# Latents' attention: the scaled copies of the keys made by ScalarE instead of VectorE

## What is computed

```python
x = x + xattn(ctx_1024, layernorm(x))   # 64 latents look at 1601 tokens and themselves, 16 heads of 64
x = x + attn(layernorm(x))              # differential attention of the latents
x = x + ffn(layernorm(x))               # 8 experts, top 2, softmax gates
```

```python
Q, K, V = (X @ W.T).reshape(b, n, 16, 16) ...   # each split in two halves of 8: Q1, Q2, K1, K2
attn = softmax(causal(Q1 K1' / sqrt(8))) - lam * softmax(causal(Q2 K2' / sqrt(8)))
O = rms_norm(attn @ V) * rms_scale * 0.2
out = O @ Wo.T
```

## Time and profile before

| | |
|---|---|
| median of three runs | 954.18 us (952.11 to 957.75) |
| the profiled execution | 957.0 us, of it a span of 955.3 us |
| TensorE busy | 914.2 us (96%) |
| VectorE busy | 800.5 us (84%) |
| ScalarE busy | 701.9 us (73%) |
| GpSimd busy | 378.7 us (40%) |
| mean granted clock of TensorE | 0.983 of full |

### The profile page before, as it was taken

The page is one execution under the profiler, slowest core; times in us unless marked ns, Lnnn a source line. Parts: engine busy times, 40 slices in busy tenths (PEclk is TensorE's granted clock), DMA queues, the critical chain, the costliest instruction groups (busy, mean ns, idle before and its releaser), DMA issues.

```text
span 955.3 us, 20495 instructions
## 1 busy us (share of the span) xinstructions
PE 914.2 (96%) x8246; PEld 491.1 (51%) x8246; DVE 800.5 (84%) x1591; ACT 701.9 (73%) x1003; POOL 378.7 (40%) x378
## 2 busy tenths in 40 slices
PE   8679999999999999999999999999999999999977
PEld 5444444545454545454545454545454545567653
DVE  5979797979798989898989898989897876498986
ACT  4756878787878787878787878787878677664633
POOL 6472034343434343434343434343434231354443
PEclk9889999999999999999999999999999999999987
DMA  6403030303030303030303030303020200000000
GB/s 213 83 1 71 1 93 2 93 2 75 22 74 21 74 22 73 22 73 22 73 23 72 23 72 24 73 23 72 23 60 23 38 23 24 1 24 24 2 2 22
DMA packets 74565, 41.95 MB, mean 44 GB/s; under 512 B 62276, under 2 KB 69864, under 8 KB 74472
## 3 DMA queue, kind: packets, MB, share of 16 engines
q1 hardware_dynamic: 74184, 39.60, 16.9%
q10 hardware_dynamic: 288, 1.05, 0.3%
HBM read 25.98 MB, written 0.59 MB: 28 GB/s over the span
## 4 chain that ended last, share of the span: by engine, by line
PE 81%; DVE 13%; ACT 3%; issue 2%; DMA 1%; POOL 0%; DVEq 0%; ACTq 0%
PE S L2141 10%; PE S L2132 9%; PE OA L2165 9%; PE OA L2168 9%; PE OA L2171 9%; PE S L2135 9%; PE WW L2075 8%; PE S L1217 2%; PE WW L2102 1%; PE WW L2103 1%; PE WW L2104 1%; DVE amx L802 1%; PE WW L2062 1%; PE WW L2063 1%; PE WW L2064 1%
## 5 line engine op out<-in xcount | busy, mean ns | idle before, releaser
L1849 ACT ACTIVATE region<-S,sigma 128x1024 f16<-128x1024 f32 x208 | 231.8, 1114 | 137.7 <-PE S L2141 137.7
L1530 DVE TENSOR_TENSOR region<-S,region 128x1024 f16<-128x1024 f32 x208 | 252.3, 1213 | 44.2 <-ACT S L1853 44.1
L1518 DVE TENSOR_REDUCE mx<-WW 128x1 f32<-128x512 f32 (+1 forms) x480 | 262.4, 583 | 29.7 <-PE WW L2075 22.4
L1853 ACT ACTIVATE S<-S,sigma 128x1024 f32<-128x1024 f32 x208 | 224.5, 1079 | 0.0
L1662 POOL TENSOR_TENSOR xk<-raw,xk 128x508 f16<-128x508 f32 x64 | 63.3, 999 | 168.1 <-DVE xk L1397 168.1
L2075 PE MATMUL WW<-xT,region 128*128 128x512 f16 x360 | 124.8, 381 | 4.4 <-DVE region L1509 2.1
L2132 PE MATMUL S<-region,xT 128*128 128x512 f16 (+1 forms) x416 | 124.5, 380 | 2.4 <-DVE region L1530 1.7
L2165 PE MATMUL OA<-region,xk 128*128 128x512 f16 (+1 forms) x416 | 123.8, 379 | 0.0
L2135 PE MATMUL S<-region,xT 128*128 128x512 f16 (+1 forms) x416 | 123.7, 379 | 0.0
L2141 PE MATMUL S<-region,xT 128*128 128x512 f16 (+1 forms) x416 | 123.7, 379 | 0.0
L2168 PE MATMUL OA<-region,xk 128*128 128x512 f16 (+1 forms) x416 | 123.7, 379 | 0.0
(11 more groups left out here) (314 smaller groups left out, 1836.6 us busy)
## 6 DMA issues: line engine op xcount, KB each, us to landing
raw<-ctx SPq DMA_DIRECT2D x16, 768.0 KB
rb<-inv_dram SPq DMA_DIRECT2D x16, 512.0 KB, 3.7
xT<-xk SPq DMA_TRANSPOSE x48, 3.1
left_row<-left_pT SPq DMA_DIRECT2D x48, 2.0 KB
raw<-ctx SPq DMA_DIRECT2D x16, 32.5 KB
WO_lo<-L_xattn_Wq ACTq DMA_DIRECT2D x1, 512.0 KB, 3.8
WO_hi<-L_xattn_Wkv ACTq DMA_DIRECT2D x1, 512.0 KB, 4.7
lx<-x SPq DMA_DIRECT2D x1, 512.0 KB, 7.1
```

Source lines behind the costliest of these rows:

```text
L1518: nc.vector.tensor_reduce(mx[:, r, c:c + 1], W[BANK[("m", n)]][:, 0:width], AX.X, ALU.max)\
L1530: nc.vector.tensor_tensor(p_lo[k], src, p_hi[k], ALU.subtract).then_inc(lo_done.sem, 1)
L1849: nc.scalar.activation(p_hi[k], src, ACT.Exp, scale=sigma[:, 0:1])
L1853: nc.scalar.activation(src, src, ACT.Exp, scale=sigma[:, 0:1]).then_inc(e_done.sem, 1)
```

## The change

In the six turns m = 0 to 5, VectorE no longer makes `Kx` of tile m+2. ScalarE does, right behind its copy of the queries, in four activations: each reads the 256 columns of keys from PSUM and multiplies them by one column of `pick` as a scale of one value per row. They wait for the projection and, from tile 2 on, for the scores of the tile whose buffer they overwrite. The keys of tiles 0 and 1 stay on VectorE. Nothing else moves.

```diff
+        def spread_keys(act, t):
+            wait(act, "projqk", t)
+            if t.off >= 2:
+                act.wait_ge(ta["scores"].sem, ta["scores"].upto(t.plus(-2), 1))
+            for k in range(4):
+                ins = nc.scalar.activation(Kx[t.off % 2][:, :, k, :],
+                                           W[0][:, 256:512].rearrange("p (c n) -> p c n", c=2), ACT.Copy,
+                                           scale=pick[:, k:k + 1])
+            ins.then_inc(ta["kx"].sem, 1)
+
@@ tail_vector
                 if m + 1 < TB:
                     maxima(t.plus(1), 0)
-                if m + 2 < TB:
-                    keys(dve, t.plus(2), W[0][:, 256:512])
                 if m == TB - 1:
@@ tail_scalar
                 if m + 2 < TB:
                     queries(act, t.plus(2), W[0][:, 0:256])
+                    spread_keys(act, t.plus(2))
                 if 0 < m < TB - 1:
                     values(act, t.plus(1), W[1])
```

## The result

| | before | changed kernel |
|---|---|---|
| median | 956.96 us (951.53 to 959.46, 22 runs) | 953.34 us (950.68 to 958.37, 22 runs) |
| the profiled execution | 957.0 us, span 955.3 | 951.6 us, span 949.9 |
| runs above 955.5 us | 13 of 22 | 2 of 22 |

The ratio is 0.9969 (95%: 0.9955 to 0.9982): 0.31% or 3.0 us faster, inside the forecast range and short of the 0.5% that counts as faster. But the two profiled spans differ by 5.4 us, the medians by 3.6 and the forecast was 1.5, so the number alone says little about the mechanism. The 22 times of before lie in two groups, 951.5 to 954.2 and 956.1 to 959.5, none between; 955.5 us is a line that I drew in the gap.

What follows compares the result with a forecast made beforehand. In the attention, TensorE and VectorE were taken as both full, with gains only where VectorE made TensorE idle. Gains of 1.16 + 0.21 + 0.61 = 1.98 less 0.5 gave 1.5 us off 954.18: 952.7 us, range 949.5 to 956.5.

Steps and rivals of the forecast that it cites:

- the clock's case: Rival, chance 0.14: TensorE's clock fall in the experts moves or vanishes; 5.4 us less (947), or 955 to 956.
- Turn 1 is worth 0.4: Attention turn 1: VectorE's L840 can begin 0.4 us earlier, then waits for GpSimd; turn 2 keeps the 0.4.
- turn 2's term of 1.16: Attention turn 2: with the keys early, TensorE's weigh_values is no longer held and L1179 begins 1.16 us earlier.
- the new bound: Attention turn 2: TensorE's next bound is ScalarE's copies 2 and 3, at 864.23 before and 0.4 us earlier now.
- Turns 4 and 5, 0.21 + 0.61: TensorE's wait of 0.21 us for Kx in turn 4 and of 0.61 for ScalarE's xk in turn 5 go away.
- Turn 3 gives nothing, VectorE waits 0.5 and 0.8: Attention turn 3: TensorE has no idle time, so no gain; VectorE waits 0.5 us for scores, 0.8 for weigh_values.
- The price of the spread, 0.364 each: ScalarE's new activations in the attention: 0.364 us each, 1.46 for four, each 0.47 to 0.50 long.
- The cost, 3 x 0.16 = 0.5: Attention turns 3, 4 and 5: ScalarE's late copy 0 holds TensorE 0.16 us a turn, 0.5 us in all.
- in turns 0 to 2 it falls into waits: Attention turns 0 to 2: the 0.16 us from ScalarE's lateness falls into TensorE's or VectorE's waits.
- ScalarE as the bound: Rival, chance 0.15: activations cost 0.575 us, TensorE is held 1.0 in turns 3 to 5; 956.4 us.
- VectorE as the bound all through: Rival, chance 0.06: every spread from turn 1 to 5 comes off, 5.65 us in all; 948.5 us.

Runs made afterwards that it cites:

- turn 1 alone: Kernel before, with ScalarE spreading the keys in turn 1 only and VectorE in the others: one run, 959.2 us.
- turn 2 alone: Kernel before, with ScalarE spreading the keys in turn 2 only and VectorE in the others: one run, 954.5 us.
- the kernel with one activation: Changed kernel with one activation instead of four in each key spread, the other three copies left out: one run, 954.1 us.
- eight activations: Changed kernel with each 256-column activation cut into two of 128 columns: one run, 959.4 us.
- the filled kernels: Unread transposes added in TensorE's two experts waits: kernel before 952.27 us, changed kernel 950.59, the one moving the spread only in turns 2 and 4 950.28.
- the kernel with turns 2 and 4 alone: Changed kernel, but ScalarE spreads the keys only in turns 2 and 4, VectorE in the others, waits not filled: 954.38 us, ratio 0.9968.
- turns 2 to 5: Changed kernel, but VectorE keeps the key spread in turns 0 and 1 and ScalarE does it from turn 2 on: one run, 957.1 us.
- Later experts: Changed kernel with six transposes of a constant table before the last turn's products with the values: 952.98 us, ratio 0.9983.

## Why the prediction was right, and where its steps were not

- *The total.* The forecast was a gain of 1.5 us and a time of 952.7; measured were 3.0 us by the ratio and 953.34. That the time came so near is luck, in two ways. The attention, which was to give the 1.5, gave 0.71, and the clock, held to be a rival with a chance of 0.14, gave most of the rest. And the 1.5 was taken off a median of three runs, 954.18, which was a run without the fall; over 22 runs before takes 956.96, and 1.5 off that is 955.5. The prediction sized the clock's case well (5.4 us) and gave it too little chance: it took the one profile it had for the state of every run, when the three times shown, 952.11, 954.18 and 957.75, were already some 5.6 us apart.
- *How much the clock gave.* The share of runs above 955.5 us fell from 13 in 22 to 2 in 22, by 0.50; 0.50 x 5.9 = 2.95 us, with 0.7 makes 3.65, against 2.7 between the means. (The medians are 3.62 apart, but with two groups a median moves from one to the other.) The two groups of before are 5.0 apart by their means, 952.95 and 958.00, and with 5.0 the sum is 3.2. The runs below 955.5 us average 952.95 before (9 runs) and 952.83 after (20), with a scatter of some 0.4 of the difference. So the times alone do not show the attention's 0.7; it rests on the stretches.
- *Turn 1 is worth 0.4.* Failed, and with it 0.4 of turn 2's term of 1.16. The prediction saw only the wait for L971's result and not what GpSimd does next. Measured: turn 1 alone gives 0.0, since L850 takes 1.49 beside GpSimd's L541, and turn 2 alone 0.67 where 1.16 was summed; TensorE's wait there went from 1.32 to 0.50. This wait of 0.50 for ScalarE's copy in turn 2 is where the new bound shows; the prediction had named it rightly, and had it begin 0.4 too early. (1.16 - 0.4 = 0.76; the 0.1 that is left was not looked into.)
- *Turns 4 and 5, 0.21 + 0.61.* The mechanism is right, the size too small. The 0.82 measured at turn 4 looks exact, but it has turn 4's own cost of 0.25 in it; without that cost turn 4 gives 1.07. The prediction took TensorE's wait of 0.61 for what VectorE's lateness costs, and the lateness was 0.84, which with the 0.21 makes 1.05. That 0.82 came out twice is luck: with its cost the forecast was 0.66.
- *Turn 3 gives nothing, VectorE waits 0.5 and 0.8.* Right: 0.44 and 0.76.
- *The price of the spread, 0.364 each.* Right, 0.358, and 482 ns long, within 0.47 to 0.50. The 0.40 of the Trainium skill (page ScalarE: Activation LUTs, section "What ACT_TABLE_LOAD costs") has the duration (an estimate by it is 492 ns) and too little overlap: here it is 482 - 358 = 124 ns, the page has 93.
- *The cost, 3 x 0.16 = 0.5.* Too small in two ways. A wait at copy 0 is 0.21, not 0.16, and each of turns 3, 4 and 5 pays 0.25. And "in turns 0 to 2 it falls into waits" failed for turn 0: TensorE waits 0.17 at copy 0 and VectorE's wait for `weigh_values` goes from 0.20 to 0.41, 0.21 us on the path. Together 0.21 + 0.25 + 0.25 + 0.26 = 0.97 us by the turns, 0.96 by the whole stretch of the kernel with one activation.
- *The rivals.* ScalarE as the bound was not met at 0.358, and with eight activations its mechanism appeared as described. VectorE as the bound all through is excluded: 1.67 us is what the attention gives even with ScalarE's cost nearly gone, not 5.65.
- **Open**: why the changed kernel meets the long fall so rarely. That this fall costs 5.9 us is read from the profiles, and that it needs TensorE's waits is shown by the filled kernels (0 of 30 runs above 955.5, none at a clock below 0.985; 3 of the 30 stand at 0.985 or 0.986, so a short fall is not excluded there). By the times, before had it in 55 of 86 runs over all chips, the changed kernel in 2 of 29 (3 by the clock), with the same two waits. It was in most runs of the kernel with turns 2 and 4 alone, though its experts come earlier; it also stood in the single profiles of turn 1 alone, turn 2 alone, turns 2 to 5, one activation and eight. So neither an earlier moment nor a shorter attention explains it. The short fall in one of the changed kernel's two profiles suggests that it may differ in how long the clock stays down; no run shows that. Later experts gave 4 of 12, which is unclear. The counts remain an inference from times and mean clocks, since one run of each kernel was profiled, two of the changed one.

## What to carry to other kernels

Moving work from a full engine to one with time to spare pays only in the turns where a third engine was waiting for the full one; elsewhere it only puts the new owner's later work back (turns 0, 3 and 5), or changes nothing (turn 1), so move it in those turns alone (here turns 2 and 4: 1.39 us of the attention instead of 0.71). Before counting on an earlier start of an instruction, read what the neighbour engine does in the time into which it moves. And when three runs of one kernel lie 5 us apart while a change is worth 1, first find the stretch in which they differ, and compare fixed stretches of two profiles rather than totals. A line between two groups of times belongs to the kernel for which it was drawn; each run's mean granted clock told the groups apart in a kernel whose times had moved.

## What the runs showed of the hardware

- The granted clock can go to 1.2 GHz 0.1 to 2.2 us behind a wait of TensorE of 2.05 us (nine profiles), in six of them before the next wait, and stay there for 17 us (926.1 to 943.2 before) or 6.7 us (924.2 to 930.9 in one profile of the changed kernel). That costs 5.9 or 1.9 us. Twenty-three transposes that nobody reads, 2.84 us of added work in this wait and the next, left no run of 30 with the long fall: 12 of before, 12 of the changed kernel and 6 of the one with turns 2 and 4.
- It is not sure to fall: the same two waits left it at 1.00 in the changed kernel's first profile, and the same program of before took 951.5 to 959.8 us from run to run.
- A short fall also came in turn 7 with TensorE busy for 1.92 and 2.00 of 2.00 us in the rows above, so a full row doesn't mean the upper level. It cost 1.2 us and stands in three of fourteen profiles.
- A VectorE instruction of 0.42 us took 1.08 or 1.49 beside one of GpSimd, by when it began, and ended 0.28 us behind it either way.
